# Gated scan: the low-rank rows stand four times over, so that the projections to and from them fill 128 rows and columns of TensorE

## The reference, cut to what matters

```python
xz = x @ W_in                                  # 128 -> 512
xc, z = jnp.split(xz, 2, axis=-1)
u = silu(causal depthwise conv of xc, 4 taps)  # 256 channels
xp = u @ W_x                                   # 256 -> 32
dt_raw, B_raw = jnp.split(xp, 2, axis=-1)      # 16 and 16
dt = softplus(dt_raw @ W_dt + b_dt)            # 16 -> 256
Bp = B_raw @ W_Bp                              # 16 -> 256
dt = clip(dt, 0.0001, 1.0)
ub = u * Bp
h[t] = h[t-1] * (1 - dt[t]) + ub[t]            # over 1024 tokens
y = (h + D_param * u) * silu(z)
return y @ W_out                               # 256 -> 128
```

## Time and profile before

| | |
|---|---|
| median of three runs | 3335.51 us |
| the profiled execution, own time | 3336.73 us |
| its span | 3334.4 us |
| mean granted TensorE clock over the span | 0.892 of full |
| TensorE busy, matmuls | 2652.5 us (80%) |
| VectorE busy | 2215.7 us (66%) |
| GpSimd busy | 2022.9 us (61%) |
| ScalarE busy | 1578.9 us (47%) |
| gated scan, first to last instruction | about 528 to 869 us |

### The profile page before, as it was taken

How to read it: one execution, slowest core, us unless ns; L and a number is a source line. 1 busy time by engine, 2 the same in 40 slices (tenths; PEclk the granted TensorE clock), 3 DMA queues, 4 the chain that set the end, 5 groups by cost and what they waited for, 6 DMA issues and landing times. The chain is left out here.

```text
span 3334.4 us, 43893 instructions
## 1 busy us (share of the span) xinstructions
PE 2652.5 (80%) x12400; PEld 1872.7 (56%) x12400; DVE 2215.7 (66%) x3996; ACT 1578.9 (47%) x2668; POOL 2022.9 (61%) x1643
## 2 busy tenths in 40 slices
PE   5799995999759999546997688878878775569882
PEld 4699993444639999435997233323333332459662
DVE  5656653676475665576333499999999999663333
ACT  4433333665533333234333566766667562443331
POOL 0477771222027777323674589999999885335776
PEclk9999997787579999758999799899999999589997
DMA  6111121100231111341233488888889897312333
GB/s 177 33 47 48 47 46 50 38 25 1 60 87 48 46 47 46 76 139 35 81 87 72 147 297 294 291 301 293 288 301 310 278 298 241 101 36 74 89 91 87
DMA packets 286366, 429.58 MB, mean 129 GB/s; under 512 B 58332, under 2 KB 195839, under 8 KB 286240
## 3 DMA queue, kind: packets, MB, share of 16 engines
q1 hardware_dynamic: 250784, 357.34, 32.9%
q0 software_dynamic: 35456, 70.86, 9.3%
HBM read 367.51 MB, written 62.39 MB: 129 GB/s over the span
## 5 line engine op out<-in xcount | busy, mean ns | idle before, releaser
L683 POOL DMA_INDIRECT m_rows<-rows_in,m_source x568 | 550.6, 969 | 589.6 <-SPq L580 221.9
L1588 PE MATMUL s_y_ps<-s_prod,ident 128*128 128x512 f32 x1024 | 521.9, 635 | 210.2 <-DVE s_prod L1875 210.1
L1553 POOL TENSOR_TENSOR s_dBu<-s_du,s_B_row 128x1024 f32<-128x1024 f32 x256 | 602.7, 2361 | 83.5 <-DVE s_dA L1868 70.5
L1868 DVE TENSOR_TENSOR_SCAN s_dA<-s_dA,s_dBu 128x1024 f32<-128x1024 f32 x256 | 585.6, 2287 | 44.4 <-POOL s_dBu L1553 44.4
L721 PE MATMUL m_A_ps<-m_rowsT,m_own 128*128 128x256 f32 x2272 | 570.5, 385 | 2.0 <-ACT m_rowsT L763 1.1
L737 PE MATMUL m_Y_ps<-m_own,m_hid 128*128 128x128 f32 x4544 | 556.1, 276 | 3.6 <-issue 3.6
L737 PEld LDWEIGHTS m_Y_ps<-m_own,m_hid 128*128 128x128 f32 x4544 | 531.2, 192 | 5.7 <-issue 5.6
L1588 PEld LDWEIGHTS s_y_ps<-s_prod,ident 128*128 128x128 f32 x1024 | 181.3, 196 | 520.1 <-DVE s_prod L1875 327.2
L773 ACT ACTIVATE m_act_a<-m_A_ps,m_own 128x256 f32<-128x256 f32 x568 | 238.1, 470 | 435.1 <-PE m_A_ps L721 303.6
L721 PEld LDWEIGHTS m_A_ps<-m_rowsT,m_own 128*128 128x128 f32 x2272 | 416.3, 194 | 49.0 <-ACT m_rowsT L763 1.9
L1689 ACT ACTIVATE s_dA<-s_delta,s_decay 128x1024 f32<-128x1024 f32 x256 | 286.1, 1118 | 306.7 <-DVE s_prod L1875 301.2
(11 more groups left out here) (239 smaller groups left out, 3631.7 us busy)
## 6 DMA issues: line engine op xcount, KB each, us to landing
s_B_row<-s_bc_rows SPq DMA_DIRECT2D x256, 512.0 KB, 5.7
s_C_row<-s_bc_rows SPq DMA_DIRECT2D x256, 512.0 KB, 6.0
rows_out<-m_y_sb SPq DMA_DIRECT2D x142, 128.0 KB
rows_in<-m_xs SPq DMA_DIRECT2D x64, 256.0 KB, 2.3
m_rows<-rows_in,m_source POOLq DMA_INDIRECT x568
s_got<-rows_by_token SPq DMA_DIRECT2D x16, 512.0 KB, 5.2
m_got<-rows_by_token SPq DMA_DIRECT2D x32, 256.0 KB, 4.1
rows_by_token<-m_y_sb,m_target POOLq DMA_INDIRECT x284
```

The source lines that it names most:

```text
L683: pool.indirect_dma_start(rows[:, b % AHEAD, r, :], None, c.rows_in, bass.IndirectOffsetOnAxis(source[:, 2 * b + r:2 * b + r + 1], 0)).the ...
L1553: nc.gpsimd.tensor_tensor(dBu[q % RING][:, :], du[s % 2][:, h, :], B_row[q % RING][:, :], ALU.mult).then_inc(dBu_ready, 1)
L1588: ins = nc.tensor.matmul(y_ps[:, at(cc, 512)], c.ident[:, :], prod[q % 2][:, at(cc, 512)], start=(n == 0), stop=(n == NS - 1))
L1868: nc.vector.tensor_tensor_scan(dA[q % 2][:, :], dA[q % 2][:, :], dBu[q % RING][:, :], 0.0, ALU.mult, ALU.add).then_inc(scanned, 1)
```

## The change

`w_x` is loaded four times side by side along its columns, so that the low projection gives 128 rows in PSUM: the 32 low-rank rows, four times over. `xp` becomes 128 partitions tall. `w_dt` and `w_b` become 128 rows tall too, each loaded four times, at rows 32 r (32 r + 16 for `w_b`), and both are multiplied by 1/4 once, on VectorE; so the sum over 128 rows is the sum over 32 of before. The number of matmuls is the same. The loads of the stage go from 10 to 16, there are two more VectorE instructions, and TensorE waits for these two (`wide_scaled`) before its first matmul.

```diff
+    COPIES = P // PAIR
...
-        w_x = sb("w_x", [P, HALVES, PAIR])
-        w_dt = sb("w_dt", [PAIR, INNER])
-        w_b = sb("w_b", [PAIR, INNER])
+        w_x = sb("w_x", [P, HALVES, COPIES, PAIR])
+        w_dt = sb("w_dt", [P, INNER])
+        w_b = sb("w_b", [P, INNER])
...
-        xp = sb("xp", [PAIR, SEQ])
+        xp = sb("xp", [P, SEQ])
...
-        LOADS = 10 * 16
+        LOADS = (8 + 2 * COPIES) * 16
...
-            load(w_x[:, 0, :], w["w_x"][0:P, :])
-            load(w_x[:, 1, :], w["w_x"][P:2 * P, :])
+            for h in range(HALVES):
+                load(w_x[:, h, :, :], w["w_x"][at(h, P), :].unsqueeze(1).to_broadcast([P, COPIES, PAIR]))
             sp.wait_ge(cleared, 5)
-            load(w_dt[0:NS, :], w["w_dt"])
-            load(w_b[NS:PAIR, :], w["w_b"])
+            for r in range(COPIES):
+                load(w_dt[r * PAIR:r * PAIR + NS, :], w["w_dt"])
+                load(w_b[r * PAIR + NS:r * PAIR + PAIR, :], w["w_b"])
...
             pe.wait_ge(conv_taps, CONV)
+            pe.wait_ge(wide_scaled, 2)
...
-                        ins = nc.tensor.matmul(use.ps[0:PAIR, :], w_x[:, h, :], u[t % 2][:, h, at(cc, 512)],
+                        ins = nc.tensor.matmul(use.ps[:, :], w_x[:, h, :, :].rearrange("p r n -> p (r n)"), u[t % 2][:, h, at(cc, 512)],
                                                start=(h == 0), stop=(h == HALVES - 1))
...
-                    nc.scalar.copy(xp[:, at(cc, 512)], use.ps[0:PAIR, :]).then_inc(use.free, 1)
+                    nc.scalar.copy(xp[:, at(cc, 512)], use.ps[:, :]).then_inc(use.free, 1)
...
+            for wide in (w_dt, w_b):
+                nc.vector.tensor_scalar(wide[:, :], wide[:, :], 1.0 / COPIES, None, ALU.mult).then_inc(wide_scaled, 1)
```

More of the change, by code:

```diff
@@ L941, in gated_scan @@
         free = [sem(f"bank{i}_free") for i in range(BANKS)]
-        loaded, cleared, conv_taps = sem("loaded"), sem("cleared"), sem("conv_taps")
+        loaded, cleared, conv_taps, wide_scaled = sem("loaded"), sem("cleared"), sem("conv_taps"), sem("wide_scaled")
         rows_here, added, stat_done = sem("rows_here"), sem("added"), sem("stat_done")
```

## The result

The changed kernel took 3279.56 us (median of four runs, 3278.98 to 3282.22), the kernel before beside it 3336.69 (3335.38 to 3338.61): a ratio of 0.983, 95% interval 0.9813 to 0.9847, or 57 us less. Forecast were 3277 and a range of 3270 to 3300. The profiled execution, the slowest of the four, has a span of 3279.4 us where the one before had 3334.4: 55.0 less.

What follows compares the result with a forecast made beforehand. TensorE, at a mean clock of 0.78, was taken to bound the gated scan's full period of 36.8 us. Stretches saving 62.3 us, less 3.2 of setup, gave 59.1 us and a forecast of 3277 us, range 3270 to 3300.

Steps and rivals of the forecast that it cites:

- The clock: Gated scan's TensorE: rows in use hold the clock, so full rows give 1.00 from the first rise on.
- first stretch: Gated scan up to the second project_in: full clock from w_dt on saves 5.9 us, cold start stays.
- second stretch: Next sequence, without output projection: ScalarE's loop rules, 28.2 us for 35.7, saving 7.5.
- five full periods: Repeating periods of the gated scan: 28.9 us each in place of 36.8, together 39.5 us saved.
- last stretch: End of the gated scan: 9.4 us saved, final output projection staying cold.
- start: Stage setup: six more loads on SP's queue cost 2.9 us, small w_x pieces 0.3, together 3.2 us later.
- the loop that was named: Full period: w_b product, sums, convolution, GpSimd, normalisation, copies, w_dt, transposes set 28.9 us, TensorE 0.4 behind.
- its own loop: Full period: ScalarE's work, less one row copy, plus waits for w_dt and the transposes, makes 28.2 us.
- Rival 1: Low projection of 32 columns and the gap before w_dt cause the clock's fall: 3297 us, chance 0.09.
- rival 2: Rows don't matter or the chip counts something else, clock as before: 3339 us, chance 0.05.
- rival 3: Clock as before and setup at its worst, first got load held behind 512-piece loads: 3344 us, chance 0.02.
- rival 4: Loops tighter, xp copies 1 us more or GpSimd and sums later: period 31 us, 3290 us, chance 0.12.

Runs made afterwards that it cites:

- the two half experiments: Against the kernel before: 128-row wide matmuls with added rows zero, low projection 32 columns, ratio 0.9836; 128-column low projection with 32-row wide matmuls, ratio 1.0007.
- copies-first kernel: Changed kernel with ScalarE's two xp copies put before the normalisation of the next sequence: 3270.13 us, ratio 0.9797 to the kernel before.
- the loads alone: Kernel before with the sixteen loads of the changed kernel, matmuls using only the first copy: 3585.56 us, ratio 1.0010.
- the changed kernel's second execution: The changed kernel run again, unaltered, beside the kernel before on another chip: 3278.17 us, ratio 0.9820.
- the first experiment: Kernel before with xp, w_dt and w_b 128 rows tall, the 96 added rows zero, low projection 32 columns, ten loads: 3521.54 us, ratio 0.9836.
- the last three: Changed kernel with xp copies before normalisation, 3270.13 us; that order on the zero-filled kernel, 3266.74; the latter with first got loads ahead of the weights, 3265.44.
- the first and second experiments: Kernel before with wide matmuls on 128 rows, added ones zero, 3521.54 us; kernel before with only the low projection widened to 128 columns, 3582.71 us.
- the period with zeros and 32 columns: Zero-filled rows, 32-column low projection and ten loads, with xp copies before normalisation on ScalarE: 3266.74 us, ratio 0.9786 to the kernel before.

## Why the prediction was right, step by step

**The clock.** The choice on which all hung, rows in use and not busy share, was right, and the two half experiments show it. The prediction named "full rows in `low`, `w_dt` and `w_b`" in one breath; the first of the three has no part in it. The rule of the Trainium skill set against it ("TensorE: Matmul & The Clock Gate", "Why this matters for your kernels": busy engine, full clock) does not describe this stage: the earlier trace rows has the engine busy without a pause at 0.50. Beside it, the changed kernel pauses for 1.85 us in every period of 28.87 and stays at 1.00.

**The terms.** All from the two profiled executions, in us saved:

| | forecast | measured |
|---|---|---|
| first stretch | 5.9 | 33.38 − 27.57 = 5.8 |
| second stretch | 7.5 | 35.68 − 28.06 = 7.6 |
| five full periods | 39.5 | 184.0 − 144.4 = 39.6 |
| last stretch | 9.4 | 60.33 − 51.90 = 8.4 |
| start | −3.2 | 26.25 − 32.10 = −5.85 |
| sum | 59.1 | 55.6 |

(184.0 is the time from the third `project_in` to the eighth before, 807.47 − 623.50; 144.4 the same after, 760.17 − 615.82.) The spans differ by 55.0. The period of 28.9 came out at 28.87, by the loop that was named: `w_dt` starts 21.05 us into the period where 21.0 was worked out, and ScalarE's wait of 0.42 us for the shift puts its own loop at 28.4 or so (forecast 28.2). The prediction had TensorE 0.4 behind the loop; the copies-first kernel shows 1.13. TensorE alone came to 27.74, not 28.5: its transposes took 0.87 and not 1.0, the low projection and the pause 0.5 less once the copies no longer waited, and 0.1 went with the 32 columns (below).

**What was off.** The start: "I take 0.3" for the small pieces, 3.2 in all. The price of the six issues was right (2.9; with the loads alone 3.5 in all, 29.80 us from first load to `project_in` in the changed kernel's second execution), and that of the small pieces showed nowhere; the profiled execution had 1.7 us more in one issue and 1.2 us more until `got` landed (544.71 − 537.52 = 7.2, against 538.96 − 532.98 = 6.0). The last stretch: 0.75 of the missing 1.0 us is the final output projection, whose clock rose later this time (6.75 us for 6.00 in the earlier trace rows; 5.55 to 6.72 in the experiments).

**The second stretch.** The forecast had the clock at 1.00 there and ScalarE's loop as the bound. The bound was right, the clock was not: it fell between 603 and 604 us and came back between 606 and 607, in the low projection, after a pause of 1.86 us before it. The same fall stands in the second execution of the changed kernel, and none in the first experiment and the last three, whose kernels have the same pause there (1.86 to 1.88 us). So full rows held the clock in every full period, but they are not all that decides; what does is open. The fall cost nothing: the first experiment has the same stretch without it, and the same length.

```profile
642.33:670.39 28.06, 23.63 (x62) 9.88 (x60) 23.92 (x40) 23.62 (x45) 10.19 (x4) 1.00 0.14 38
```

TensorE waits there for ScalarE either way, 0.79 us before `w_dt` in the changed kernel and 2.57 in the first experiment. That the fall came where TensorE had time to spare was luck.

**The rivals.** Rival 1 (pause and low projection) and rival 2 (clock as before) are excluded by the first and second experiments; rival 3's price (a load of small pieces holding `got` back by microseconds) did not show; rival 4's period of 31 us was not reached.

## What to carry to other kernels

A stream of matmuls that contracts over few rows can pay twice: not in its own time at full clock, which is the same, but by halving the clock for itself and for what follows it. Where the granted clock is 0.5 under a busy TensorE, look at the rows its operands use; here rows of zeros in both operands were enough, and they needed one more memset but no loads, no copies and no scaling. Then look for what is late next: here two instructions changed places on one engine were worth another 8 us, seen from the one wait that had appeared before the matmuls.

## What the runs showed of the hardware

- The clock followed the rows that the instructions name, not what is in them: with 96 of 128 rows zero in both operands it was 1.00 for 220 us, with 32 rows 0.78 on average. No run separates the rows themselves from something else that comes with them in such an instruction.
- 64 rows are not simply enough or too few: the same instructions lost the clock in three sequences and kept it in five.
- At full clock a 128x512 record takes the same time whatever its shape (592 ns with 32 columns, 587, 589 and 592 with 32, 64 and 128 rows), but the change of shape does not come free. The timeline of PE from z to the low projection, before:

```profile
674.85 3.60 PE L1076 MATMUL s_bank<-s_xnT,s_w_in 128*128 128x512 f32 x8
678.38 3.62 PE L1095 MATMUL s_bank<-s_u,s_w_x 128*32 128x512 f32 x8
```

and in the changed kernel, where the start of z is:

```profile
656.86 3.60 PE L1079 MATMUL s_bank<-s_xnT,s_w_in 128*128 128x512 f32 x8
```

The eight z records take 678.38 − 674.85 = 3.53 us ahead of a projection of 32 columns, 660.30 − 656.86 = 3.44 ahead of one of 128; and the period with zeros and 32 columns is 27.85 us where that with 128 columns is 27.74. The Trainium skill ("TensorEngine Tiling (Array Packing)", "Key Properties") says that changing the tiling mode drains the engine. A tenth of a microsecond at such a change agrees with it, though no run here shows that a drain is what takes it. With 64 rows, at a clock of 1.00, there are more such changes:

```profile
805.14 1.09 PE L1090 MATMUL s_bank<-ident,s_xn 128*128 128x128 f32 x8
806.16 3.70 PE L1109 MATMUL s_bank<-s_xp,s_w_b 64*128 64x512 f32 x8
809.79 1.99 PE L1072 MATMUL s_bank<-s_xnT,s_w_in 128*128 128x512 f32 x4
```

The transposes take 806.16 − 805.14 = 1.02 us where 128 rows have 0.87, `w_b` 809.79 − 806.16 = 3.63 for 3.44. From `w_dt` to the end of the period it is 809.79 − 801.54 = 8.25 us for 673.57 − 665.75 = 7.82, which is the extra third of a microsecond of that kernel's periods and a little more.
